# Scaled, negated attention scores and a one-instruction bias for the exponential

## The reference

```python
queries = x @ Wq.T + bq
keys = content_embeddings @ Wk.T + bk
values = content_embeddings @ Wv.T + bv
scale = 1.0 / sqrt(256)
scores = einsum('bqc,bkc->bqk', queries, keys) * scale
attn = softmax(scores, axis=-1)
attended = einsum('bqk,bkc->bqc', attn, values)
out = (x + attended) @ Wo.T + bo
```

## Time and profile before

| | |
|---|---|
| median of 3 runs | 1036.92 us (1036.11 to 1036.98) |
| profiled execution | 1036.67 us |
| its span in the profile | 1034.5 us |
| busy VectorE / TensorE | 894.5 / 925.0 us |
| busy GpSimd / ScalarE | 852.8 / 756.4 us |

### The profile page before, as it was taken

The page is one execution under the profiler, slowest core; times in us unless marked ns, Lnnn a source line. Parts: engine busy times, 40 slices in busy tenths (PEclk is TensorE's granted clock), DMA queues, the critical chain, the costliest instruction groups (busy, mean ns, idle before and its releaser), DMA issues. The chain is left out here.

```text
span 1034.5 us, 13058 instructions
## 1 busy us (share of the span) xinstructions
PE 925.0 (89%) x4158; PEld 488.3 (47%) x4192; DVE 894.5 (86%) x1216; ACT 756.4 (73%) x1323; POOL 852.8 (82%) x616
## 2 busy tenths in 40 slices
PE   8886988999989999899989999899989999867896
PEld 6642453545435453545435454545435454423454
DVE  1635888899989999899989999899989999899965
ACT  2356657877797859877797859877797869666555
POOL 1059998899979898899979898898979898899920
PEclk9998989999999999999999999999999999989999
DMA  9804710445042610545043610535033400500000
GB/s 354 333 34 163 289 59 2 162 147 202 0 150 99 243 42 2 183 143 205 0 128 115 246 44 2 184 125 223 2 109 120 161 0 2 184 0 0 1 21 21
DMA packets 21915, 116.33 MB, mean 112 GB/s; under 512 B 3479, under 2 KB 4119, under 8 KB 9304
## 3 DMA queue, kind: packets, MB, share of 16 engines
q1 hardware_dynamic: 16232, 80.70, 21.2%
q10 hardware_dynamic: 5616, 34.81, 9.4%
HBM read 111.04 MB, written 4.46 MB: 112 GB/s over the span
## 5 line engine op out<-in xcount | busy, mean ns | idle before, releaser
L1172 DVE TENSOR_TENSOR_SCAN state<-decay,state 128x512 f32<-128x512 f32 (+1 forms) x352 | 590.5, 1696 | 35.3 <-ACT decay L932 22.8
L861 POOL TENSOR_TENSOR state<-w,brep 128x512 f32<-128x512 f32 (+1 forms) x352 | 612.5, 1771 | 0.5 <-POOL w L894 0.4
L1326 PE MATMUL acc<-state,ident 128*128 128x512 f32 x832 | 412.3, 612 | 15.7 <-DVE state L1172 13.8
L932 ACT ACTIVATE decay<-delta,neg_a 128x496 f32<-128x496 f32 x512 | 329.6, 669 | 89.7 <-DVE state L1172 88.6
L1326 PEld LDWEIGHTS acc<-state,ident 128*128 128x128 f32 x832 | 148.5, 193 | 165.5 <-issue 111.9
L869 POOL TENSOR_TENSOR state<-state 128x512 f32<-128x512 f32 x96 | 122.2, 1273 | 45.8 <-DVE state L1172 44.3
L1326 PE MATMUL bank<-xn_t,in_w 128*128 128x512 f32 x128 | 62.0, 618 | 5.0 <-DVE u L1318 3.4
L1326 PE MATMUL bank<-out_w,u 128*128 128x256 f32 x256 | 58.2, 383 | 8.7 <-DVE u L1159 8.7
L916 ACT ACTIVATE soft<-x_in,nmr,rstd 128x256 f32<-128x256 f32 x64 | 33.2, 589 | 42.9 <-POOL nmr L825 42.9
L966 ACT ACTIVATE sg<-bank,ag 128x512 f32<-128x512 f32 x64 | 43.6, 681 | 24.0 <-PE bank L1326 23.1
L894 POOL TENSOR_TENSOR w<-delta,u 128x512 f32<-128x512 f32 x32 | 39.9, 1269 | 22.7 <-ACT delta L1068 22.7
(11 more groups left out here) (170 smaller groups left out, 1318.2 us busy)
## 6 DMA issues: line engine op xcount, KB each, us to landing
keys<-in_keys_t SPq DMA_DIRECT2D x32, 1028.0 KB, 6.0
brep<-b_scratch ACTq DMA_DIRECT2D x32, 1024.0 KB, 6.8
keys<-in_keys_n SPq DMA_DIRECT2D x29, 1024.0 KB
out<-x_in SPq DMA_DIRECT2D x16, 256.0 KB, 5.0
x_in<-in_x SPq DMA_DIRECT2D x14, 256.0 KB
u<-in_keys_n SPq DMA_DIRECT2D x1, 1024.0 KB
w<-in_keys_n SPq DMA_DIRECT2D x1, 1024.0 KB
delta<-in_keys_n SPq DMA_DIRECT2D x1, 1024.0 KB
```

The source lines that it names most:

```text
L861: nc.gpsimd.tensor_tensor(state[g % CPT][:, 0:count * tok].rearrange("p (c t) -> p c t", c=count), w[:, m, 0:tok].unsqueeze(1).to_broadcas ...
L932: last = nc.scalar.activation(decay[:, q:q + groups * GSEQ, 1:LEN], d, ACT.Exp, scale=neg_a[:, m, n + i:n + i + 1])
L1172: nc.vector.tensor_tensor_scan(flat, by, flat, 0.0, ALU.mult, ALU.add).then_inc(scan_done, 1)
L1326: return nc.tensor.matmul(o, l, r, start=first, stop=last)
```

## The change

The matrix `qk_w`, `q_bias`, `kb_col` and `kb_const` are multiplied by -1/16 as VectorE takes them out of PSUM. So scores and `kb` come out of TensorE already scaled, and negative. The row's maximum becomes the minimum of these numbers, the exponential's scale becomes -1, and the bias is `(mx + kb) - kb` in one instruction with two per-partition scalars, both the same column of `kb`. The part `s_neg` with its tile, its semaphore and its entries in the tables is gone; `s_bias` stays where it was and now waits for the reduce itself.

```diff
-    ("s_neg", [14, 17, 27, 35]),
...
-                                             bias=ebias[:, g:g + 1], scale=SCALE,
+                                             bias=ebias[:, g:g + 1], scale=-1.0,
...
             def qk():
                 dve.wait_ge(prep_mm, 1)
-                nc.vector.tensor_copy(qk_w[:, :, :].rearrange("p h d -> p (h d)"), bank[:, A, :])
-                nc.vector.tensor_copy(q_bias[:, :], acc[:, 0:HALVES])
-                nc.vector.tensor_copy(kb_col[:, :], acc[:, 4:4 + HALVES])
-                nc.vector.tensor_copy(kb_const[:, :], acc[:, 8:9]).then_inc(w_ready, 1)
+
+                for to, of in ((qk_w[:, :, :].rearrange("p h d -> p (h d)"), bank[:, A, :]),
+                               (q_bias[:, :], acc[:, 0:HALVES]), (kb_col[:, :], acc[:, 4:4 + HALVES]),
+                               (kb_const[:, :], acc[:, 8:9])):
+                    last = nc.vector.tensor_scalar(to, of, -SCALE, None, ALU.mult)
+                last.then_inc(w_ready, 1)
...
-                        nc.vector.tensor_reduce(mx[:, one], bank[:, att_banks(g, scan)[0], 0:KEYS], AX.X, ALU.max)\
+                        nc.vector.tensor_reduce(mx[:, one], bank[:, att_banks(g, scan)[0], 0:KEYS], AX.X, ALU.min)\
                             .then_inc(max_done, 1)
-                    elif part == "s_neg":
+                    elif part == "s_bias":
                         one = slice(g, g + 1)
                         reach(dve, kb_ready, b, 1)
                         reach(dve, max_done, b, g + 1)
-                        nc.vector.tensor_scalar(nmx[:, one], mx[:, one], kb[:, one], -SCALE, ALU.add, ALU.mult)\
-                            .then_inc(nmax_done, 1)
-                    elif part == "s_bias":
-                        one = slice(g, g + 1)
-                        reach(dve, nmax_done, b, g + 1)
-                        nc.vector.tensor_scalar(ebias[:, one], kb[:, one], SCALE, nmx[:, one],
-                                                ALU.mult, ALU.add).then_inc(ebias_ready, 1)
+                        nc.vector.tensor_scalar(ebias[:, one], mx[:, one], kb[:, one], kb[:, one],
+                                                ALU.add, ALU.subtract).then_inc(ebias_ready, 1)
```

More of the change, by code:

```diff
@@ L109 @@
     ("turn2", [69]),
-    ("s_neg", [7, 8, 19, 29]),
     ("query", [0]),
@@ L148 @@
     ("stats1", [0]),
-    ("s_neg", [15, 19, 23, 32]),
     ("times_u", [82, 83, 87, 87]),
@@ L527, in perceiver_layer @@
         mx = sb("mx", [P, GROUPS])
-        nmx = sb("nmx", [P, GROUPS])
         ebias = sb("ebias", [P, GROUPS])
@@ L603, in perceiver_layer @@
         max_done = sem("max_done", 1, 1)
-        nmax_done = sem("nmax_done", 1, 1)
         ebias_ready = sem("ebias_ready", 1, 1)
```

## The result

Over 20 runs of each kernel the changed one has a median of 1031.47 us and the kernel before 1034.21 us; the ratio is 0.9977, with a 95% interval of 0.9968 to 0.9987. That is 2.4 us less (1.3 to 3.3), where the prediction had 3.3 us less. Only 3 of the 20 runs of before lay ahead of the prediction, with a median of 1036.92 us; against all 20 the base was 2.7 us lower. The profiled execution of the changed kernel took 1032.31 us, with a span of 1030.5 us.

The account below looks back on a forecast made before the run. Bound: a loop over VectorE, TensorE, then VectorE, GpSimd and ScalarE, the change lying in its VectorE part. 3.0 us from six blocks plus 0.3 from block 1: 1036.67 - 3.3 = 1033.4, against the median 1033.6 us; range 1031.6 to 1036.3.

Parts of the forecast that it names:

- The nine tenths: Share of the six steady blocks' 3.3 us expected to reach the end, 3.0 us; the rest ends at late neighbours.
- s_neg at 0.71 us a block: Removing s_neg shortens VectorE's queue in a steady block by 0.25, 0.12, 0.23 and 0.11 us in groups 0 to 3.
- The forecast of VectorE's busy time: In the profile after, VectorE's busy time in a block was to fall by 0.63 us.
- The second scalar: s_bias reading two per-partition scalars costs 0.04 us more each, 0.16 us a block, bounds 0 and 0.09 each.
- The sum of a block: Net gain of 0.55 us in a steady block, 3.3 us in six blocks.
- Block 1: 0.3 us: In block 1, half of 0.6 us counted because VectorE soon stops for ScalarE; bounds 0 and 0.6.
- Rival 5: Granted clock falls at a few more places, 1.0 us a stretch, three undo the gain: 1036.9 us; chance 0.05.
- Rival 1: TensorE takes the gain in the steady blocks, at most a third passes: 1035.6 to 1036.9 us; chance 0.15.
- Rival 2: A link costs only an unlinked instruction's price, groups 0 and 2 give 0.12 us each: 1035.0 us; chance 0.05.
- Rival 4: Reduce by minimum dearer than by maximum on VectorE's path in 24 groups, up to 1043 us; chance 0.05.
- The start's constants under cover: At the start, four qk evacuations become multiplications; 1.8 us of cover hides any extra, counted nothing, upper bound 0.9 us.
- block 0 at nothing: In block 0 TensorE's wait for the last group's keys hides the gain; counted nothing, at most 0.2 us.

Follow-up runs that it names:

- two_steps: Changed kernel with the bias again made by two linked instructions of one scalar and one constant each, in their old places: block distance 116.47 us, changed kernel 116.14.
- neg_g0_linked: Changed kernel with s_neg put back for group 0 in the steady blocks, the bias waiting for it besides its two other waits: block distance 116.51 us against 116.14.
- neg_g0_link_alone: Changed kernel with s_neg put back for group 0 in the steady blocks, the bias waiting for it alone: block distance 116.40 us against 116.14.
- two_constants: Changed kernel with the bias as mx times 1.0 plus 0.0, two constants and no per-partition scalar: block distance 115.84 us against 116.14.

## Why the prediction was right, and where it was off

**The bound.** VectorE sets the pace in the stretch in which the bias is made, and TensorE had room. Right: 0.11, 0.25 and 0.26 us put in there came out at the end of the block in full, and VectorE's wait at the sums stayed at 2.3 us in all these runs. The nine tenths that I let through were too few; what is really on VectorE's path passes whole.

**The term that was mis-sized: s_neg at 0.71 us a block.** The groups 0 and 2 were right (0.25 and 0.23; measured 0.25 and 0.26). The groups 1 and 3, 0.12 and 0.11 us by the distance to the next start, are worth nothing and 0.02. In group 1 the distance to the next start was the wrong measure: the successor was waiting for the instruction in front of both. That the 0.12 us read there, which the prediction also took as the price of an instruction without a wait, comes close to the 0.11 us measured for one is chance. In group 3 the next scan but one was waiting for a decay. So the sum is 0.53 us of the 0.71. The forecast of VectorE's busy time went wrong in the same way: it fell from 109.78 to 109.45 us a block, 0.33 and not 0.63, since a short instruction overlaps its neighbours (s_neg at 336.68 starts before `gate` has ended at 336.76).

**The second scalar.** Forecast 0.16 us a block from the difference of two durations, 0.04 us a bias and four of them; measured 0.17 us, but as 0.06 in three groups. Right by size, and in part by luck: too little for one bias, and one group too many.

**The sum of a block.** 116.14 + 0.25 + 0.26 + 0.02 - 0.17 = 116.50 us, where before had 116.48: the experiments account for the whole steady gain. Six blocks give 2.0 us, not 3.3 less a tenth. The total couldn't have shown this: its interval of 1.3 to 3.3 us holds both these 2.0 us and the 3.3 us of the forecast.

**Block 1: 0.3 us.** No gain is to be seen there. Up to x1 GpSimd goes through this block without a stop, and it releases x1 with its own addition. Its timeline before, then after:

```profile
99.88 2.35 POOL L861 TENSOR_TENSOR state<-w,brep 128x1024 f32<-128x1024 f32 x1
...
139.14 2.38 POOL L829 TENSOR_TENSOR x_in<-x_in,vo_row 128x1024 f32<-128x1024 f32 x1
```

```profile
98.44 2.34 POOL L855 TENSOR_TENSOR state<-w,brep 128x1024 f32<-128x1024 f32 x1
...
137.69 2.39 POOL L823 TENSOR_TENSOR x_in<-x_in,vo_row 128x1024 f32<-128x1024 f32 x1
```

From the one to the end of the other it is 41.64 us in both. I had read GpSimd as behind VectorE in the steady block and took that over to block 1, where it isn't so; that VectorE waited there 1.7 us for GpSimd at x1 stood in the trace.

**The profile's own difference.** The two profiled executions differ by 4.4 us. Windows over block 1 before, after and in two_steps:

```profile
102.89:213.45 110.56, 99.27 (x402) 50.06 (x402) 92.59 (x111) 78.53 (x142) 103.61 (x74) 0.95 0.33 120
```

```profile
102.62:209.70 107.08, 96.52 (x401) 49.19 (x401) 91.92 (x108) 77.76 (x141) 102.33 (x73) 0.97 0.33 124
```

```profile
101.40:209.30 107.90, 96.20 (x402) 49.20 (x402) 92.36 (x111) 78.46 (x142) 103.47 (x74) 0.98 0.33 123
```

3.5 us lie in block 1, at a granted clock of 0.95 against 0.97. The kernel with two bias instructions also took 107.9 us there, at 0.98, and three kernels with the change (neg_g0_linked, neg_g0_link_alone, two_constants) took 109.5 to 109.7 us at 0.95, so this is the clock of one execution and not the change. That is likely also why the 20 times of the two kernels scatter by 4.5 and 7.8 us. Rival 5 acts in both directions and in both kernels.

**Rivals.** Rival 1 is excluded for this change; what stops the next one is on TensorE's side too, but it is a wait of its queue for ScalarE. Rival 2 gave a period 0.2 to 0.35 us shorter, into which the measured 0.34 falls, but by another way: the link has its full price, and two instructions have none. The Trainium skill ("VectorE: DVE Perf Modes", section "The DRAIN you can't avoid") says, from eight tensor_copy with and without semaphores, that a semaphore between two VectorE operations costs nothing extra. For one-column instructions this doesn't hold: a link costs at least 0.15 us (116.40 against 116.25). The prediction also left out the section's exception, that a next operation that isn't held starts earlier; the unlinked bias, 0.13 us behind the start of a 0.21 us s_neg, agrees with that. Rival 4 is excluded, 411 ns both. The start's constants under cover and block 0 at nothing are borne out as far as the profiles show: the kb column of block 0 starts at 22.27 us and the one of block 1 at 102.62, 80.35 us later, where it was 80.4 (22.50 to 102.89).

## What to carry to other kernels

The distance to the next start prices a small instruction only if its successor waits for nothing else: look at what the successor needs, and whether the instruction stands inside that wait. Price links and waits, not only instructions, and take off waits that another one covers. Before counting on a gain further on, look at what the queue of the next engine waits for: work taken out of TensorE's queue only made it wait longer for ScalarE. Where the total scatters by more than the effect, measure the period of the steady loop: differences of 0.1 us show in it, in single profiles.

## What the runs showed of the hardware that was not expected

- Waits that are already met can cost VectorE time: two of them in front of the wait of a linked one-column instruction cost 0.11 us (116.51 against 116.40), one in front of the wait for the reduce 0.06 us (116.14 against 116.08). Behind an instruction still in work, with no link, two cost at most 0.02 us (0.13 against 0.11 us from start to start).
- Each per-partition scalar of a one-column instruction costs about 0.06 us of its duration: 142 ns with two constants, 203 with one scalar, 263 with two (means of 32).
- Without the one-column matmuls of kb the mean granted clock of an execution was 0.973 to 0.980, with them 0.980 to 0.987 (12 runs each), and the whole took 2.6 us more (medians 1032.88 and 1030.25).
